# Graph attention on one core: transposed one-hots made on ScalarE, queries three groups ahead, one TensorE signal a group

## The reference

```python
Qh = (x @ Wq.T + bq).reshape(n, H, D)     # Kh, Vh alike; H = 4 heads of 16
Ee = (edge_attr @ We.T + be).reshape(-1, H, D)
score = (Kh[src] * Qh[dst] * (1.0 / np.sqrt(D)) * Ee).sum(-1)
score = jnp.exp(jnp.clip(score, -5.0, 5.0))
msg = Vh[src] * score[..., None]
wV = jax.ops.segment_sum(msg, dst, num_segments=n)
x = layernorm(x + wV.reshape(n, H * D))
```

## Time and profile before

| | us |
|---|---|
| median of 3 runs | 14131.57 |
| lowest and highest run | 14116.25, 14145.13 |
| span of the profiled execution, first to last instruction | 13943.9 |
| attention stage within it (8413 to 13900) | 5487 |
| busy in the whole span: PE, PEld | 7881.3, 6966.0 |
| busy in the whole span: DVE, ACT, POOL | 5002.0, 2112.3, 7746.7 |

### The profile page before, as it was taken

One profiled execution on the slowest core, in us unless ns is written; L12 is line 12 of the kernel. 1 busy time (PEld: TensorE's weight loads), 2 busy tenths in 40 slices (PEclk: granted clock), 3 DMA queues, 4 the chain that ended last, 5 costly groups with the idle time before them and its releaser, 6 DMA issues.

```text
span 13943.9 us, 198796 instructions
## 1 busy us (share of the span) xinstructions
PE 7881.3 (57%) x55262; PEld 6966.0 (50%) x55263; DVE 5002.0 (36%) x11869; ACT 2112.3 (15%) x4676; POOL 7746.7 (56%) x8220
## 2 busy tenths in 40 slices
PE   4566656565665556556655565445555555555554
PEld 4555545555554444455545454444444444444454
DVE  3333333333333233333333334333333334333334
ACT  1111111111111000000000012222222222222222
POOL 5555655555555555655555556555555555555554
PEclk7766766766676666666666675555555555555555
DMA  3222222222222111121111112222222222222221
GB/s 62 55 50 52 54 54 50 51 50 49 50 48 49 41 44 42 42 45 42 40 43 40 39 43 65 61 59 59 59 58 57 57 56 56 56 55 53 54 53 51
DMA packets 861613, 712.24 MB, mean 51 GB/s; under 512 B 474896, under 2 KB 730544, under 8 KB 860544
## 3 DMA queue, kind: packets, MB, share of 16 engines
q0 software_dynamic: 260000, 369.16, 12.3%
q1 hardware_dynamic: 515345, 225.59, 6.8%
q10 hardware_dynamic: 85325, 105.63, 2.2%
HBM read 584.55 MB, written 115.24 MB: 50 GB/s over the span
## 4 chain that ended last, share of the span: by engine, by line
another core or an unknown queue 41%; PE 25%; issue 18%; DVE 8%; DVEq 4%; ACT 3%; ACTq 1%; POOL 0%; DMA 0%; POOLq 0%; SPq 0%
PE ps_kv L727 4%; PE ps_kv L718 3%; PE ps_e L704 3%; PE ps_sum L889 2%; PE ps_sum L687 2%; PE ps_q L687 2%; PE ps_hot L687 2%; ACT node_q L1014 1%; PE ps_t L696 1%; DVE score L1484 1%; DVE ps_t L1481 1%; PE ps_kv L736 1%; DVE attention_space L1482 1%; DVEq L420 1%
## 5 line engine op out<-in xcount | busy, mean ns | idle before, releaser
L591 POOL DMA_INDIRECT kv<-kv_rows,src_ids x3125 | 2948.0, 943 | 2512.3 <-DVE message L1490 1659.0
L591 POOL DMA_INDIRECT kv<-in_x,src_ids x2500 | 2358.9, 944 | 1805.8 <-issue 924.5
L591 POOL DMA_INDIRECT kv<-h_rows,src_ids x2500 | 2360.9, 944 | 1761.2 <-issue 917.3
L889 PE MATMUL ps_sum<-message,node_h 128*128 128x64 f32 x6260 | 1475.2, 422 | 272.3 <-DVE message L1490 259.1
L889 PEld LDWEIGHTS ps_sum<-message,node_h 128*128 128x128 f32 x6260 | 1402.7, 332 | 304.5 <-DVE message L1490 285.4
L718 PE MATMUL ps_kv<-between,hot 128*128 128x490 bf16 x2500 | 883.4, 500 | 975.2 <-ACT node_q L1014 618.3
L687 PE MATMUL ps_sum<-kv,hot 128*128 128x65 f32 x5000 | 940.6, 355 | 262.3 <-issue 219.3
L687 PEld LDWEIGHTS ps_sum<-kv,hot 128*128 128x128 f32 x5000 | 924.4, 277 | 286.7 <-issue 286.1
L687 PE MATMUL ps_hot<-kv 128*128 128x65 f32 x1880 | 412.7, 396 | 1041.6 <-issue 900.3
L687 PEld LDWEIGHTS ps_hot<-kv 128*128 128x128 f32 x1880 | 385.2, 306 | 1115.1 <-issue 1113.1
L718 PEld LDWEIGHTS ps_kv<-between,hot 128*128 128x128 bf16 x2500 | 289.5, 129 | 1293.6 <-issue 995.4
(11 more groups left out here) (242 smaller groups left out, 11227.5 us busy)
## 6 DMA issues: line engine op xcount, KB each, us to landing
node_q<-in_edge_attr SPq DMA_DIRECT2D x125, 480.0 KB
edge_space<-ee_rows SPq DMA_DIRECT2D x125, 480.0 KB
kv<-kv_rows,src_ids POOLq DMA_INDIRECT x3125
kv<-in_x,src_ids POOLq DMA_INDIRECT x2500
node_q<-in_edge_attr SPq DMA_DIRECT2D x125, 320.0 KB
kv<-h_rows,src_ids POOLq DMA_INDIRECT x2500
edge_space<-ee_rows SPq DMA_DIRECT2D x125, 320.0 KB
ee_rows<-node_q ACTq DMA_DIRECT2D x25, 1440.0 KB
```

The source lines that it names most:

```text
L591: nc.gpsimd.indirect_dma_start(out=into_slot, out_offset=None, in_=table_rows, in_offset=bass.IndirectOffsetOnAxis(ap=ids, axis=0),).then_ ...
L889: mm = nc.tensor.matmul(to, one_hots[:, k, :], messages[:, k, :], start=(k == 0), stop=(k == K - 1))
```

## The change

In words:

- **No transposes.** SP loads the 640 destinations of a group into every partition (`edge_ids`, a broadcast of 2,560 bytes to each of 128 partitions), five groups deep. ACT makes the turned one-hot itself: the square of (destination − node of this partition), then ReLU of one minus that, written into `hotT[:, u]`. `turn_hots`, ACT's copy out of `ps_hot`, and ACT's widening of `hot` are gone; DVE writes its one-hot straight into `hot32` as float32.
- **Queries three groups ahead** (QUERIES = 3). There are five query banks, one a slot, in place of three; ACT prepares `hotT` and `q_block` four groups ahead.
- **A sum in a later query's bank.** The message sum of g-1 goes into 64 columns of the bank of group g+3, just before the queries of g+3, and DVE adds it when it comes to group g+3.
- **One TensorE signal a group**: `query` of g+3 covers both. `hot_t` and `summed` are gone (one `summed` stands at the very end). An extra has two signals, `x.query` and `x.summed`, in place of three.

The core of the diff:

```diff
+QUERIES = 3
-        ps_query = (ps_q, ps_kv[:, 512:1024], ps_q, ps_kv[:, 512:1024], ps_e)
+        ps_query = (ps_q, ps_kv[:, 512:1024], ps_e, ps_kv[:, 0:512], ps_sum)
+        ps_node = [bank[:, K * D:(K + 1) * D] for bank in ps_query]
...
+                def load_ids(g, u):
+                    sp.dma_start(edge_ids[:, u, :], dst[bass.ds(g * GE, GE)].rearrange("(o e) -> o e", o=1).to_broadcast([P, GE])).then_inc(p.ids[u], 16)
+                def reload_ids(g, u):
+                    sp.wait_ge(p.hot_c, g + 2)
+                    load_ids(g + SLOTS, u)
...
-                        turn_hots(p, g + 1, following)
                         pe.wait_ge(p.message, g + SLOTS)
-                        sum_messages(ps_sum[:, 0:D], hot32[:, (u - 1) % SLOTS], message[:, (u - 1) % SLOTS], p.summed)
-                        queries(p, g + 1, following, g + 1)
-                        extra_queries(p, x, words[u + 2], following)
-                        extra_sums(x, words[u], (u - 1) % SLOTS)
+                        sum_messages(ps_node[(u + QUERIES) % SLOTS], hot32[:, of], message[:, of])
+                        extra_sums(x, words[u], of)
+                            pe.wait_ge(p.scored, g + 1)
+                            queries(p, x, g + QUERIES, (u + QUERIES) % SLOTS, words[u + QUERIES + 1])
...
-                act.wait_ge(p.query, g)
-                nc.scalar.copy(q_block[:].rearrange("p (a f) -> p a f", a=1), node_q[:, bass.ds(block_at(first), 1), :])
-                act.wait_ge(p.hot_t, g + 1)
-                nc.scalar.copy(hotT, ps_hot[:, 0:K * P].rearrange("p (i j) -> p i j", i=K)).then_inc(p.hot_c, 1)
-                nc.scalar.copy(hot32[:, u], hot[:, u])
+            def block_edges(apart, into, ids, b, done, count, ready):
+                nc.scalar.activation(apart, ids, ACT.Square, bias=opposite[:, bass.ds(b, 1)]).then_inc(done, 1)
+                act.wait_ge(done, count)
+                nc.scalar.activation(into, apart.rearrange("n (e k) -> n k e", k=K), ACT.Relu, bias=unit[:], scale=-1.0).then_inc(ready, 1)
...
-                    one_hot(g + 2, block_at(words[u + 3][1]), hot[:, then], p.hot)
-                    extra_hots(words[u + 2], g + 1)
-                    dve.wait_ge(x.added, words[u][0] + 1)
-                    dve.wait_ge(p.summed, g + 1)
-                    add_sums(words[u][1], ps_sum[:, 0:D])
+                        one_hot(g + 1, block_at(words[u + QUERIES + 2][1]), hot32[:, (u + 1) % SLOTS])
+                    dve.wait_ge(x.added, words[u + QUERIES][0] + 1)
+                    add_sums(words[u][1], ps_node[u])
```

More of the change, by code:

```diff
@@ L354, in __init__ @@
                     self.ee = [sem(f"att_ee{i}") for i in range(len(PARTS))]
-                    self.hot_t = sem("att_hot_t")
+                    self.ids = [sem(f"att_ids{u}") for u in range(SLOTS)]
+                    self.apart = sem("att_apart")
                     self.hot_c = sem("att_hot_c")
@@ L380, in __init__ @@
             def __init__(self):
[L382 removed]
+                self.apart, self.hot_c = sem("x_apart"), sem("x_hot_c")
                 self.query = sem("x_query")
@@ L545, in feed_attention @@
                                 load_sources(part, T + 1, 2 * (2 * BIG + T + 1) + part, SLOTS, 0)
-                with sp.Fori(TURNS - SUBS + 1, TURNS) as t:
-                    products(t)
+                with sp.Fori(TURNS - SUBS, TURNS - 2) as t:
+                    turn(t, SLOTS)
+                turn(TURNS - 2, SLOTS - QUERIES)
             load_edges(0)
@@ L861, in layer_two @@
                 keys_values_queries(CHUNKS - 1)
-            def turn_hots(p, g, u):
-                pe.wait_ge(p.hot, g + 1)
-                hold(pe)
-                for k in range(K):
-                    tp = nc.tensor.transpose(ps_hot[:, k * P:(k + 1) * P], hot[:, u, k, :], ident16[:])
-                tp.then_inc(p.hot_t, 1)
             def query_rows(to, turned, block_rows):
@@ L877, in query_rows, with queries @@
                 return mm
-            def queries(p, g, u, scored):
-                pe.wait_ge(p.scored, scored)
+            def queries(p, x, g, u, word):
                 pe.wait_ge(p.hot_c, g + 1)
                 nc.tensor.matmul(ps_query[u][:, 0:K * D], ones16[:], zeros16[:], start=True, stop=False)
-                query_rows(ps_query[u], hotT, q_block)
-            def sum_messages(to, one_hots, messages, done):
-                for k in range(K):
-                    mm = nc.tensor.matmul(to, one_hots[:, k, :], messages[:, k, :], start=(k == 0), stop=(k == K - 1))
-                mm.then_inc(done, 1)
-            def extra_queries(p, x, word, u):
+                query_rows(ps_query[u], hotT[:, u], q_block[:, u])
                 before, first, more = word
@@ L895, in extra_queries, with sum_messages @@
                     with pe.Fori(0, more) as j:
-                        n = before + j
-                        pe.wait_ge(x.hot, n + 1)
-                        for k in range(K):
-                            tp = nc.tensor.transpose(ps_hot[:, k * P:(k + 1) * P], hot_x[:, k, :], ident16[:])
-                        tp.then_inc(x.hot_t, 1)
-                        pe.wait_ge(x.hot_c, n + 1)
+                        pe.wait_ge(x.hot_c, before + j + 1)
                         query_rows(ps_query[u], hotT_x, q_block_x).then_inc(x.query, 1)
                 nc.tensor.matmul(ps_query[u][:, 0:1], ones16[:], zeros16[:, 0:1], start=False, stop=True).then_inc(p.query, 1)
+            def sum_messages(to, one_hots, messages):
+                for k in range(K):
+                    mm = nc.tensor.matmul(to, one_hots[:, k, :], messages[:, k, :], start=(k == 0), stop=(k == K - 1))
+                return mm
             def extra_sums(x, word, u):
@@ L1144, in _ @@
             v.memset(zero[:], 0.0)
+            v.memset(unit[:], 1.0)
             v.memset(attr[:, :, K * D:], 0.0)
@@ L1497, in add_sums @@
                 return v.tensor_tensor(nodes, nodes, sums.rearrange("p (o f) -> p o f", o=1), ALU.add)
-            def extra_hots(word, g):
-                before, first, more = word
-                with dve.If(more):
-                    with dve.Fori(0, more) as j:
-                        n = before + j
-                        dve.wait_ge(x.query, n + 1)
-                        hold(dve)
-                        one_hot(g, block_at(first + j + 1), hot_x, x.hot)
             def extra_sums(word, g):
@@ L1516, in extra_sums, with score_turn @@
                         b = block_at(first + j + 1)
-                        one_hot(nc.s_assert_within(g, 0, G - 1, skip_runtime_bounds_check_because="the table's first word is 0"), b, hot32_x, x.hot32)
+                        one_hot(nc.s_assert_within(g, 0, G - 1, skip_runtime_bounds_check_because="the table's first words are 0"), b, hot32_x).then_inc(x.hot32, 1)
                         dve.wait_ge(x.added, n + 1)
                         dve.wait_ge(x.summed, n + 1)
-                        add_sums(b, ps_extra[:, 0:D]).then_inc(x.added, 1)
-            words = group_words(ENG.DVE, 0, 0, 2)
-            for u in range(2):
-                one_hot(u, block_at(words[u][1]), hot[:, u], p.hot)
-            extra_hots(words[0], 0)
-            with dve.Fori(0, TURNS) as t:
-                words = group_words(ENG.DVE, t, 1, SLOTS + 3)
+                        add_sums(b, ps_extra).then_inc(x.added, 1)
+            def score_turn(t, last):
+                words = group_words(ENG.DVE, t, QUERIES + 1, QUERIES + 1 + SLOTS + 1)
                 for u in range(SLOTS):
```

158 lines of the change are left out of this document (97 added, 61 removed).

## The result

The changed kernel takes 13,874.14 us (median of 4 runs, 13,854.44 to 13,878.78), the kernel before in the same comparison 14,133.35 us (14,116.25 to 14,145.13). The ratio is 0.9815, 95% interval 0.9801 to 0.9829. The forecast was 13,500 us (12,950 to 13,850): right in sign, 2.4 times too large in the saving, and the result lies 24 us outside the range.

A forecast was written before the change was run, and what follows sets the result against it. The prediction took POOL's gathers plus one stall a batch to bound the attention: 625 groups falling from 5474 to 4841 us save 633, other terms about nothing, so 14131.57 − 633 gives about 13,500 us, range 12,950 to 13,850.

The forecast's parts named there:

- TensorE's signals come late: Attention: while POOL gathers without a break, PE's signals arrive late, most only after the batch and a tail.
- n = 5: Attention: after a stall DVE gets far enough for five groups in each unbroken batch of POOL's gathers, against 1.826 before.
- n = 4 without a slip. Each slip adds a group: Attention batch length: four groups from durations alone; each PE signal that gets through during a batch adds one.
- The stall for n = 5: POOL's stall after a five-group batch: between 6.9 and 8.6 us, taken as 7.5; 7.745 us a group, 633 us saved.
- growth by 0.72 us a group: Attention: the delay of signals after a batch's last gather grows 0.143 us a gather, 0.72 us a group.
- Transposes and their copy: Attention: PE loses five matmuls a group, ACT 0.69 and 0.71 us; behind the signals' delay worth nothing.
- ACT's two operations: ACT's new square and ReLU over 640 columns: 1.4 us together, at most 2.5 us should one double; hidden.
- DVE and edge ids: Attention: DVE's float32 one-hot costs nothing extra (878 against 880 ns); SP's 625 added id loads, 204.8 MB, cost 0 us.
- Rival 5: Attention slower: id loads take longer than a group, so ACT and DVE wait; at 9.5 us a load 14,600 us; chance 0.07.
- the 187.7 us: Whole kernel: the excess of the median time over the profiled span of 13943.9 us, left unchanged in the forecast.
- Rival 3: Attention: an extra's sum or fewer slipped-through signals keep batches near three groups; 8.6 us a group, 14,040 us; chance 0.12.
- Rival 1: Attention: signals get through in time and POOL never stops, 6.245 us a group; saves 1571 us, about 12,560; chance 0.10.

The follow-up runs named there:

- i1_direct_small_ids: Changed kernel with SP's plain loads of the same 640 rows replacing POOL's attention gathers, and id reloads cut to 16 partitions by 64 bytes: 11,374.72 us, ratio 0.8037.
- e4_pause: Changed kernel, with POOL clearing 600 unused columns and waiting for that after each group's five gathers in the attention: 13,488.74 us, ratio to before 0.9535.
- e2_queries1: Changed kernel with queries made one group ahead instead of three (QUERIES = 1): 14,008.95 us, ratio to before 0.9917.
- e3_no_extras: Changed kernel without the extra blocks' work in the attention (97 second node blocks in 625 groups left out): 13,692.99 us.
- e1_small_ids: Changed kernel with each attention reload of edge ids cut to 16 partitions by 64 bytes, from 128 by 2,560: 13,892.01 us.

## Why the prediction was wrong in size

**What bounds the kernel.** Right for the late condition: gathers plus one stall a batch are the stage, after as before. That the gathers make the others late is shown by i1_direct_small_ids, where they are gone while the first two stages are as slow as ever. That a break shortens the stalls is shown by e4_pause, on this one kernel. Too narrow was "TensorE's signals come late": DVE's, ACT's and PE's own instructions do too. The trace of before hid that. Its batches rarely outlast 10 gathers, but length isn't all: e2_queries1 has batches as short, and PE and ACT stand at "issue" for 1656 and 966 us. It is likely that before they stood waiting for signals at those times and had nothing to issue; no run separates this.

**The step that failed: n = 5.** Measured 2.34. It was put together as "n = 4 without a slip. Each slip adds a group", with DVE at 3.54 us a group whatever POOL does. 150 of the 267 batches are 15 gathers, three groups; only 4 are longer. The trace shows two things in those 150, where the prediction had the fourth group done on time:

- The fourth group's queries were to be sent 2.1 us after DVE's start, with POOL idle. PE ended them 4.3 us after it in the median, 0.2 us after POOL's restart, so that in 64 batches they beat the restart and in 86 they didn't. In those 86 DVE began the group 20.9 us after the restart in the median, when the batch of 18.4 us was over.
- In the 64 where they were sent in time, DVE still began its products 9.7 us after the restart, in 62 of them with "issue" before it, and from there to the end of the message took 11.6 us (medians), not 3.54. The message came 3.6 us after the batch's last gather.

So the step takes DVE's pace from the idle time into the batch, where DVE's own instructions are late, and half of the time PE is too late for it as well. Only in 4 batches did anything add a group to the three. With one group of distance most batches are two groups (249 of 347), with three most are three: two more groups of distance made the usual batch one group longer. The other 113 batches are one or two groups. Without extras 47 are, and n is 2.78 (e3_no_extras), so extras cut n from 2.78 to 2.34 as the prediction feared; the 181 us are what that is worth, their own work included.

**The stall for n = 5.** 7.5 us forecast, 5.23 measured net at n = 2.34. From below the prediction's rule gives 4.59 + 0.72 × (2.34 − 1.82) = 4.96 us there, so the mean fits. The growth by 0.72 us a group behind it isn't borne out: after batches of one, two, three and four groups POOL is idle for 4.87, 7.39, 5.24 and 7.94 us in the mean. That the mean comes out is in part luck.

**Transposes and their copy: "worth nothing".** Wrong as a term. With the distance at one group the changed kernel is 125 us under the one before (e2_queries1). That is what the removed signals, transposes and copies and the moved sum are worth together; no run splits them.

**ACT's two operations.** 0.82 and 1.44 us against 0.7 each; the ReLU is inside its upper bound of 2.5, and hidden in every run, even where a group takes 4.5 us.

**DVE and edge ids.** 880 ns as before; ids 0 us as taken (e1_small_ids), DMA share 0.35 against "near 0.4". Rival 5 has no case.

**The sum against 14,131.57.** The step that left the 187.7 us between span and median as they are was most likely wrong, as told above: the profiled execution seems to have been about 190 us faster than the timed ones. Between the two traces the attention's gathers take 160 us less, between the medians 259 are saved: the rest would lie in what that one execution had spared, and no trace of before at the timed pace splits it.

**Rivals.** Rival 3 (short batches, n near 3, 8.6 us a group; 13,780 to 14,100 us; over 200 waits, many behind the extra's add) is what happened, given 0.12: 8.48 us a group, 247 waits, 77 of DVE's at an extra's add. Its cause was put as extras and fewer slips; extras account for 2.34 against 2.78, and from there to 5 it is the fourth group and the slips that didn't come. Rival 1 (gathers never stop, 6.245 us a group) is exactly the prompt condition, but there the kernel before does it too, so that nothing is saved. The Trainium skill's 26 ns a signal ("TensorE: Matmul & The Clock Gate", section "The cost: per-tile semaphore tail") would make the removed signals 33 us. The trace doesn't agree with it as the whole price in the late condition: one wait of 24.8 us stands in the waits after, and the changed kernel with one group of distance saves 125 us.

**Which kernel to keep.** Of the complete kernels measured in the late condition the changed one with the pause is best (13,489), in the prompt one either kernel without it (10,456 and 10,460); there the pause costs 7%. What the pause does to the kernel before in the late condition was never measured.

## What to carry to other kernels

Before a stall is modelled, measure the same kernel on several occasions: here two conditions 35% apart decided what the change was worth (1.85% or nothing), and a stall that looked like part of the program was there in only one. An engine that hands out indirect gathers without a break can hold up all the others; a test that costs one line is a pause in it, and if the kernel gets faster, the bound isn't that engine's work. And a duration read while an engine is undisturbed (here DVE's 3.54 us a group) must not be carried into a stretch where the trace shows others late: the queries were sent in time in 64 batches of 150, and the group still wasn't done.

## What the hardware showed that was not expected

- Two conditions for one and the same program, 10,443 to 10,461 and 14,134 to 14,146 us, and both (10,443 and 14,146) on chips that the record gives one number. Gathers (945 ns), their spacing of 1.25 us within a batch and the granted clock in the attention (0.50 to 0.53) are alike in both.
- In the late condition, matmuls of one run with no wait in it start up to 2.8 us apart on PE while POOL gathers (2675 us of "issue" in the stage). Without gathers it is gone (170 us, i1_direct_small_ids); with a break after every five gathers it is not (2019 us, e4_pause), though POOL's stalls are far fewer.
- ACT's ReLU over 640 columns, read as float32 with a stride of 20 bytes and written as bf16, takes 1444 ns; the square of 640 integers without a stride 825; the copy of 640 that was taken away 690. Which property costs the rest, no run tells.
